# Where VectorE and ScalarE activate u in the first chunk of an attention + FP4 FFN kernel

## The reference, cut to what matters

```python
x_proj = silu(x @ W1 + b1)
u, v, q, k = split(x_proj, 4)                 # each (2048, 128)
attn = silu(q_h . k_h) / 2048                 # 16 heads, 2048 x 2048, no softmax
av = attn @ v_h
y = layernorm(av * u, gamma, beta) @ W2 + b2
x1 = layernorm(x + y)
h = silu(fp4(x1) @ fp4(w_gate).T) * (fp4(x1) @ fp4(w_up).T)    # 352 wide
out = layernorm(x1 + fp4(h) @ fp4(w_down).T)
```

## Time and profile before

| | |
|---|---|
| median of three runs | 512.57 us |
| the profiled execution | 512.54 us |
| its span | 510.4 us |
| PE busy | 493.1 us (97%) |
| ACT busy | 483.7 us (95%) |
| DVE busy | 359.0 us (70%) |
| POOL busy | 94.8 us (19%) |

### The profile page before, as it was taken

How to read it: one execution, slowest core, us unless ns; L and a number is a source line. 1 busy time by engine, 2 the same in 40 slices (tenths; PEclk the granted TensorE clock), 3 DMA queues, 4 the chain that set the end, 5 groups by cost and what they waited for, 6 DMA issues and landing times.

```text
span 510.4 us, 20579 instructions
## 1 busy us (share of the span) xinstructions
PE 493.1 (97%) x9110; PEld 267.5 (52%) x9112; DVE 359.0 (70%) x874; ACT 483.7 (95%) x541; POOL 94.8 (19%) x204
## 2 busy tenths in 40 slices
PE   8899999999999999999999999999999999999995
PEld 5453344444444445444444445444477777777762
DVE  7643833878879787887879788787978583435445
ACT  4899999999999999999999999999999999999940
POOL 8414001002110401113020211113030402112020
PEclk9999999999999999999999999999999999999999
DMA  4734100001000010001000010001000000000000
GB/s 129 192 92 127 32 1 3 1 3 33 8 3 1 13 28 8 1 8 34 1 8 2 8 32 8 3 2 34 7 9 4 24 19 10 9 4 10 4 8 10
DMA packets 18630, 11.88 MB, mean 23 GB/s; under 512 B 2199, under 2 KB 18206, under 8 KB 18542
## 3 DMA queue, kind: packets, MB, share of 16 engines
q1 hardware_dynamic: 17256, 8.86, 6.7%
q0 software_dynamic: 704, 1.33, 1.0%
q10 hardware_dynamic: 582, 0.40, 0.3%
HBM read 1.92 MB, written 1.05 MB: 6 GB/s over the span
## 4 chain that ended last, share of the span: by engine, by line
PE 48%; ACT 28%; DVE 12%; issue 10%; DMA 1%; POOL 1%; POOLq 0%; DVEq 0%; SPq 0%
PE ps L477 46%; ACT attn L741 27%; DVE xn_b L992 2%; DVE hqT_b L987 2%; PE ps L491 2%; DMA q_stack<-parts 1%; DVE gate_b L1007 1%; DVE hqT_b L985 1%; DVE xn_b L982 1%; DVE gate_b L978 1%; DVE hqT_b L989 1%; DMA gate_b<-in_L_attn_b 1%; DVE gate_b L1046 1%; POOL rstd_b L427 0%; DVE hqT_b L981 0%
## 5 line engine op out<-in xcount | busy, mean ns | idle before, releaser
L741 ACT ACTIVATE attn<-ps 128x1024 f32<-128x1024 f32 x512 | 472.6, 1176 | 1.6 <-PE ps L477 1.4
L477 PE MATMUL ps<-attn,v_pad 128*32 128x256 f32 (+1 forms) x5120 | 274.4, 341 | 0.9 <-DVE hqT_b L1065 0.2
L477 PEld LDWEIGHTS ps<-attn,v_pad 128*32 128x32 f32 x5120 | 132.2, 109 | 81.2 <-issue 36.5
L477 PE MATMUL ps<-q_stack,k_stack 64*128 64x256 bf16 (+1 forms) x2560 | 166.7, 251 | 7.1 <-DMA q_stack<-parts 1.3
L477 PEld LDWEIGHTS ps<-q_stack,k_stack 64*128 64x128 bf16 x2560 | 81.3, 94 | 114.6 <-ACT attn L741 71.1
L426 POOL TENSOR_TENSOR ve_a<-mv_a,eps_col 128x1 f32<-128x1 f32 x24 | 4.6, 191 | 192.8 <-DVE mv_a L910 192.8
L426 POOL TENSOR_TENSOR ve_b<-mv_b,eps_col 128x1 f32<-128x1 f32 x24 | 4.6, 192 | 191.3 <-DVE mv_b L910 191.3
L477 PE MATMUL ps<-zeros 128*128 128x512 bf16 x49 | 13.6, 418 | 1.4 <-DVE zeros L1082 1.2
L970 DVE COPY xqT<-ps 128x128 f32<-128x128 f32 x15 | 4.4, 292 | 13.8 <-PE ps L477 13.8
L427 POOL TENSOR_TENSOR rstd_a<-ve_a,minus_half 128x1 f32<-128x1 f32 x24 | 13.5, 564 | 1.9
L427 POOL TENSOR_TENSOR rstd_b<-ve_b,minus_half 128x1 f32<-128x1 f32 x24 | 13.5, 562 | 1.9
(11 more groups left out here) (215 smaller groups left out, 476.8 us busy)
## 6 DMA issues: line engine op xcount, KB each, us to landing
q_stack<-parts SPq DMA_DIRECT2D x44, 64.0 KB, 2.1
k_stack<-parts SPq DMA_DIRECT2D x12, 128.0 KB, 3.0
k_stack<-parts SPq DMA_DIRECT2D x15, 64.0 KB, 2.7
q_stack<-zeros SPq DMA_DIRECT2D x14, 64.0 KB, 2.7
x_sb<-in_L_attn_x SPq DMA_DIRECT2D x3, 256.0 KB, 4.5
k_stack<-parts POOLq DMA_DIRECT2D x9, 64.0 KB, 2.6
out<-x_a SPq DMA_DIRECT2D x8, 64.0 KB, 1.6
out<-x_b SPq DMA_DIRECT2D x8, 64.0 KB, 2.1
```

The costliest lines, as they stand in the source:

```text
L477: return pe.matmul(to, lhsT, rhs, start=start, stop=stop, skip_group_check=True)
L741: return act.activation(to, frm, ACT.Silu, **kw)
```

## The change

- ("u", 0) is made 256 wide in place of 512, at step 10 in place of 12.
- ("u", 256) is a new job at step 13. ("q", 256) goes from step 14 to 15.
- ("u", 1792) is a new job at step 24, in place of the late job at step 206.
- w2 goes from step 24 to 27, gate from 26 to 29, up from 28 to 31, down from 30 to 32. The next job, late 0, stays at step 33.
- The three u jobs of chunk 0 are taken and activated by DVE: a new function `activate_u`, called for 0 and 256 behind the split of k 1792 and ahead of the wait for the weight loads, and for 1792 behind the quantising of w_down and ahead of w2's copies.
- ACT no longer activates any u. The other late jobs stay where they were.

```diff
-               12: ("u", 0), 14: ("q", 256), 24: ("w2", 0), 26: ("gate", 0), 28: ("up", 0), 30: ("down", 0)}
+               10: ("u", 0), 13: ("u", 256), 15: ("q", 256), 24: ("u", 1792), 27: ("w2", 0), 29: ("gate", 0),
+               31: ("up", 0), 32: ("down", 0)}
...
-            6: ("q", 1280), 7: ("u", 1280), 8: ("q", 1536), 9: ("u", 1536), 10: ("q", 1792), 11: ("u", 1792)}
+            6: ("q", 1280), 7: ("u", 1280), 8: ("q", 1536), 9: ("u", 1536), 10: ("q", 1792)}
...
-    LATE_AT = {t: BEGIN[t // 2 + 1] + (1 if t % 2 == 0 else 17 if t < WIDE else 14) for t in LATE}
+    LATE_AT = {t: BEGIN[t // 2 + 1] + (17 if t % 2 else 1) for t in LATE}
...
-                if kind in ("k", "q", "v", "u") or (kind == "gate" and tile is not None and tile not in BY_VEC)]
+                if kind in ("k", "q", "v") or (kind == "gate" and tile is not None and tile not in BY_VEC)]
...
-                    last = project(bank, kind, i * CH, CH)
+                    last = project(bank, kind, i, LW)
...
-                if kind == "u":
-                    return silu(uT[:, c * CH:(c + 1) * CH], ps[:, bank, :], bias=b1_col[:, 0:1])
...
+            def activate_u(start):
+
+                r = ROWS[1]
+                x, n, f, spare = r.gate[:, 0:LW], r.magic[:, 0:LW], r.xn[:, 0:LW], uT[:, start:start + LW]
+                bank = wait_made("u", start, None)
+                dve.tensor_scalar(x, ps[:, bank, 0:LW], b1_col[:, 0:1], X_MIN, ALU.add, ALU.max).then_inc(job_by_vec, 1)
+                wait_taken("u", start, None)
...
+                link(dve.reciprocal(f, spare))
+                link(dve.tensor_tensor(spare, x, f, ALU.mult))
...
             split("k", 1792)
+            activate_u(0)
+            activate_u(256)
             dve.wait_ge(w_loaded, 16 * W_LOADS)
             quantise_rows(wgate_n)
...
             fp4(Blocks(blocks, blocks, P, NBF, ROWS[0]), wq_ready)
+            activate_u(1792)
 
             bank = wait_made("w2", 0, None)
```

More of the change, by code:

```diff
@@ L789, in job @@
                 act.wait_ge(job_made, k + 1)
-                if (kind, i) == ("u", 0):
-                    act.wait_ge(b1_ready, 2)
                 if tile is None:
@@ L1102, in zero_v @@
                 dve.memset(v_pad[:, c * TPC:(c + 1) * TPC, :, :], 0.0).then_inc(v_zeroed, 1)
+            def activate_u(start):
[4 more added lines that the diff above has]
+                wait_taken("u", start, None)
+                link(dve.tensor_scalar(n, x, -LOG2_E, Y_MIN, ALU.mult, ALU.max))
+                link(dve.tensor_scalar(spare, n, ROUND, None, ALU.add))
+                link(dve.scalar_tensor_tensor(out=f, in0=spare, scalar=ROUND, in1=n,
+                                              op0=ALU.subtract, op1=ALU.subtract))
+                link(dve.tensor_scalar(n.bitcast(U32), spare.bitcast(U32), 23, None, ALU.logical_shift_left))
+                link(dve.scalar_tensor_tensor(out=spare, in0=f, scalar=POWERS[4] / LAST, in1=f, op0=ALU.add, op1=ALU.mult))
+                for power in (3, 2, 1):
+                    link(dve.scalar_tensor_tensor(out=spare, in0=spare, scalar=POWERS[power] / LAST, in1=f,
+                                                  op0=ALU.add, op1=ALU.mult))
+                link(dve.scalar_tensor_tensor(out=spare, in0=spare, scalar=POWERS[0] / LAST, in1=n,
+                                              op0=ALU.add, op1=ALU.mult))
+                link(dve.tensor_scalar(spare, spare, LAST, 1.0, ALU.mult, ALU.add))
+                link(dve.reciprocal(f, spare))
+                link(dve.tensor_tensor(spare, x, f, ALU.mult))
             split("k", 0)
```

## The result

The changed kernel takes 515.82 us, the median of six runs (515.44 to 517.02), against 512.55 of six runs of the kernel before (512.11 to 513.66). The ratio is 1.0068, 95% interval 1.0055 to 1.008: slower by 3.3 us, twice what was forecast and outside the range. The profiled execution took 515.86 us with a span of 513.9.

A forecast was written before the change was run, and what follows sets the result against it. The prediction took ACT's queue of activations plus late scores as the bound; -0.57 + 0.3 + 2.4 + 0 - 0.5 = +1.6 on 512.54 gave 514.2 us, range 513.2 to 515.6.

The forecast's parts named there:

- What bounds the kernel: Attention part: ACT's queue of work sets the time, 0.918 us per activation, plus the few places where a score comes late.
- Step 1: Start of chunk 0: ACT loses the 512-wide u activation, which nothing hid; -0.57 us.
- step 2: Job u 0 at step 10 waits behind v's activation, making ACT late; +0.3 us, bounds 0.2 and 0.6.
- Step 3: DVE's list in chunk 0: 6.8 us per u piece, weights start 4.9 late, w2's copies end at 75.0.
- Step 4: Step 29: PE waits 2.6 us at job gate for w2's bank, delaying ACT; +2.4 us, bounds 2.0 and 2.9.
- the three jobs in a row: Jobs up, down and late 0 at steps 31 to 33: taken as 0, upper bound 0.4 us.
- The clock: PE's pause at job gate, put at 2.3 us, should leave the clock at 2.4 GHz; nothing added to the sum.
- rival C: The clock falls in PE's pause at job gate, costing 2.5 us more over two steps; total 516.7, chance 7%.
- Step 5: Step 206 loses its job, so PE's and DVE's late chain near tile 11 starts earlier; -0.5 us, bounds 0 and -0.83.
- The sum: All terms together give +1.6 us on the profiled 512.54, so 514.2; chance 75%.
- A: DVE's work is hidden and the wait at job gate does not come; -0.8, so 511.8 (at best 511.1), chance 5%.
- B: The wait at job gate is shorter, or PE regains more from step 206 on; total within 1.0 of before, 513.0, chance 13%.

The follow-up runs named there:

- the first experiment: The changed kernel with u 1792 left as a late job at step 206, u 0 and u 256 still by DVE; 511.33 us, ratio 0.998.
- the interleaved kernel: The changed kernel with w2 at step 25, u 1792 at 27 and computed in two pieces around gate's copy, x_sb addition put off to tile 0; 510.49 us, ratio 0.9969.

## Why the prediction was wrong

By its own steps:

**What bounds the kernel.** Right. Every difference in time within the attention part shows as ACT idle or as lateness between two activations.

**Step 1** (-0.57) and **step 2** (+0.3). Right: -0.57, and PE idle 0.39 on v_sb ahead of u 0 with ACT 0.25 late at number 22. u 256 and q 256 were hidden.

**Step 3** (DVE's list). Right to 0.2: w2's copies end at 74.77 + 0.36 = 75.1, forecast 75.0.

**Step 4** (the wait at job gate, +2.4). The mechanism is right: place, releaser and length (PE idle 2.69, forecast 2.6). With the clock held up it makes ACT 2.64 late against 2.4, so the term was sized right as far as it went, inside its bounds. What it left out is the clock. I took 0.44 from scores to activation and 0.45 for job gate, at full clock; they were 0.65 and 0.78, which makes the wait 3.20, and then 0.59 and 0.23 followed. The zero for the three jobs in a row was 0.25 even at full clock, within its bound of 0.4.

**The clock.** This is the step that failed. The prediction argued from the earlier trace rows that PE's pause would leave the level at 2.4 GHz, and put nothing for it into the sum; rival C had 7%. In its place the pause of 2.69 us was followed by a granted clock of 0.50 for 3.4 us, worth 1.4 us. The row showed an average of 0.98 in a stretch at the end of the span, that is, one fall near the stretch's end. PE's last matmul had ended at 506.5, so that fall came 3.8 us behind it. One such row does not say that a pause of 2.6 (in this place the prediction wrote 2.3) is harmless. The changed kernel shows it in its own tail, which has the same instructions: its last matmul ends at 510.0, and the clock is at 1.00 until 511.4 and then

```profile
511.60:513.90 2.30, 0.00 (x0) 0.00 (x0) 0.29 (x1) 0.00 (x0) 0.00 (x0) 0.50 0.10 29
```

so it fell some 1.5 us behind the last matmul, less than half of the 3.8. The longest pauses of PE that left the clock at 1.00 were 0.67 and 1.33 us in the profile of before, 1.72 in that of the first experiment (ahead of its first scores) and 1.75 with four zeros; 2.69 was followed by a fall, and so was 3.13 in the kernel with u behind w2. The Trainium skill, "TensorE: Matmul & The Clock Gate", section "Why this matters for your kernels", warns of this with its rule on idle gaps between bursts; the trace agrees with it in kind, and the prediction should have given it far more than 7%. Rival C's price, 2.5, was too high. It had two whole steps at the lower level, 6.2 us, where the stretch lasted 3.4: PE lost 1.4 in it, and ACT lost all of that.

**Step 5** (-0.5). Right: numbers 412 to 424 take 0.51 less in all kernels in which step 206 has no job, and what they took before in the two in which it has. ACT's timeline beside the earlier trace rows: the idle rows of 0.18 and 0.22 are both gone, and 24 activations in 22.38 us have 0.37 of excess left.

```profile
392.68 22.48 ACT L742 ACTIVATE attn<-ps 128x1024 f32<-128x1024 f32 x24
415.06 0.46 ACT L742 ACTIVATE gate_b<-ps 128x352 f32<-128x352 f32 x1
```

**The sum.** 514.2 without the clock; the kernels with zeros in the pause, which are the changed kernel without that, measured 514.38 and 514.55. Their ACT stretch is 2.2 and 2.3 above before where the sum had 1.6: 0.2 more at number 60, 0.25 for the jobs in a row, and 0.3 in chunk 5, for which no term stood. The range ended at 515.6, below the 515.82, because it left C out. The sum with all bounds at their upper end, 515.9, would have covered 515.82, but by longer work on DVE and not by the clock; that would have been luck. The direction was right, the size half.

**Rivals.** A (511.8: the wait does not come) did not happen, but its sum without the wait, -0.8, is what the interleaved kernel's stretch gave, -0.85, once its order had taken the wait away. (The first experiment's 511.33 lies near A's 511.8 too, but it keeps the job at step 206, and that is luck of the start: its stretch is 0.34 shorter.) Its lower figure, 511.1, is a slip: -0.57 + 0.2 - 0.83 gives 511.3. B did not happen. C did, in the profiled execution at least.

## What to carry to other kernels

- Where one engine takes results out of a buffer that the next job needs, add up its list to each taking, not to its end: two insertions that are free alone can cross the line together. Put the taking first and the computing in the gaps, and check every later taking too, or the wait only moves.
- When a forecast contains a pause of TensorE longer than any that the trace shows at full clock, carry the lower clock in the sum, with the matmuls of some 3.4 us at the slower pace (0.85 for 0.52, 1.75 for 1.07 here), and expect the fall in some executions and not in others; a few multiplications of zeros ahead of the wait tell the two losses apart.
- What lies in engine time on the bounding engine is gained to the digit (0.57 here), once nothing else waits.

## What the runs showed of the hardware

- The granted clock fell to 0.50 at the end of a 2.69 us pause of PE, stayed there for 3.4 us and cost 1.4 us, more than the 0.57 and 0.51 together that the change takes off ACT. Behind a pause of 3.13 us it fell 1.4 us after PE had resumed. Four multiplications of zeros, 0.81 us of rows, kept it at 1.00 in the profiled execution.
- Executions of one kernel differ ahead of the first attn activation. In the first experiment's profile that activation starts at 13.92, in before's at 14.93. The cause stands in PE's timelines of the two, before's row first:

```profile
5.67 1.91 PE L477 MATMUL ps<-xT,w_qk 128*128 128x256 f32 x4
5.28 1.03 PE L478 MATMUL ps<-xT,w_qk 128*128 128x256 f32 x4
```

The same four matmuls take 1.91 in before's profile and in the other eight, and 1.03 in the first experiment's: by their pace, PE came to the full clock earlier there. The granted clock is given as 1.00 for 4 to 8 us in both profiles, so at the start of the span the column does not tell the level. Spans fall into two groups 1.1 us apart, as these two starts would make them (the short kind was profiled once, so this stays an inference): of 30 executions of before, 11 lie at 509.1 to 509.8 and 19 at 510.0 to 511.0; of the interleaved kernel's 12, seven at 508.3 to 508.6 and five at 509.4 to 509.6. Group against group the interleaved kernel gains 0.9 to 1.0, which agrees with the 0.85 of ACT's stretch; its median's 1.8 holds the luck of having more executions in the short group. The first experiment's -1.1, where ACT's stretch says -0.34, is the same: seven of its ten are in the short group.
- Some profiled executions lose 0.3 us in a chunk: chunk 5 in the changed kernel and in those with zeros, gate at 30 and u behind w2, chunks 2 and 4 with only u 1792 moved, none in the others. With only u 1792 moved, DVE sat between two neighbouring instructions at one such place, bn_stats ending at 174.29 and bn_aggr starting at 174.72, 0.43 where 0.08 is usual, and PE's job behind came late. In the others no such place was found on DVE, and what holds it there was not tried.
